# Folding the bias keys into the query weights on TensorE instead of on GpSimd and VectorE

## The chip, the cores and the metric

The kernel runs on one core of one Trainium2 chip. The metric is the device time of one execution in microseconds; lower is better. Before the change the median of three timed runs is 1137.2 us (1136.54 to 1137.88).

## What is computed

The reference is a chain of four cross-attention layers over a state `x` of 2 x 256 rows of 256 numbers and a context of 2 x 512 rows. The layer that matters here is L1: it holds two attentions of 16 heads of width 128, and each attention appends one learned "bias key" and "bias value" to the keys and values of every head.

```python
qh = (q_in @ wq + bq).reshape(b, q_len, H, K)          # H = 16 heads, K = 128
kh = jnp.concatenate([kh, jnp.broadcast_to(bias_k, (b, 1, H, K))], axis=1)
logits = jnp.einsum('bqhk,bthk->bhqt', qh, kh) / scale
```

The logit of the bias key is `q . bias_k[h]`, and `q` is linear in the layer's normed input. So a 256 x 16 matrix with one column per head, `folded[d, h] = sum_k wq[d, h, k] * bias_k[h, k]`, gives these logits from the input directly. It is needed once for each of the two attentions, and it depends on weights alone.

## The kernel before

The program is written by hand as a row of phases. Each phase owns its SBUF tiles and semaphores and ends in a barrier of all engines (line 131): nothing of the next phase, no load either, starts before the last instruction of this one. The phases are: transposes of the context, the narrow attention `L0a`, the MLP `L0m`, the two wide attentions `L1a` (more than half of the time), the MLP `L1m`, the narrow attention `L2a`, the narrow attention `L3a` and the MLP `L3m`.

The change lies in `L0m`, one of three phases that the function `mlp` writes. TensorE's work in `mlp` is a list of jobs, each into one of four PSUM banks in turn (the class `Ring`). Jobs 0 and 1 transpose the normed rows. Then come eight "up" jobs (m = 0 to 7), each six matmuls of 512 columns (lines 72 to 74) from the first weight matrix. ScalarE applies the gelu to each bank (`activated`, L849); VectorE splits the result into a high part (`hidden_hi`, a cast, L870) and a low part (`hidden_lo`, a subtraction, L871), and the second one frees the bank. Up job m may start only when VectorE has freed the bank of up job m - 4. Then come four "down" jobs, t = 0 to 3, of 24 matmuls of 256 columns each, and VectorE adds each to `x_rows` (L890). Every engine runs its own instructions strictly in order.

`L0m` alone also has the task of making `folded` for the next phase (`cfg["fold"]`, class `BiasKeyFold`). The query weights of an attention (2 MB) and its bias keys, broadcast over the 128 partitions (1 MB), are loaded; `fold.multiply` takes the product in place in pieces of 128 x 2048 (three pieces on GpSimd, the fourth on VectorE, L914), and `fold.reduce` on VectorE sums each piece over the width of a head (L919). VectorE's four reductions and its multiply stand between its MLP instructions. `L3m` is the same MLP with the same shapes, without the fold and without this neighbour work.

A second piece of code matters for reading the change. In the phase `L0a` the bias values are folded into the output weights by TensorE already: a tile `spread` of zeros, 32 columns per head, receives the head's vector in column c (L610); then 32 float32 matmuls of 32 weight columns and 256 moving columns (L435) put the 16 heads of each layer on four strips of 32 PSUM partitions.

Of the kernel before, what the change touches and what calls it, by code (L numbers as in the profile page):

```python
# [10 lines left out]
ALU = mybir.AluOpType  # L11
# [3 lines left out]
P = 128  # L15
# [3 lines left out]
D = 256  # L19
# [23 lines left out]
class Ring:  # L43


    def __init__(self, banks, sem, name):
        self.banks = banks
        self.n = len(banks)
        self.full = sem(f"{name}_full")
        self.hi_done = sem(f"{name}_hi_done")  # L50
        self.free = [sem(f"{name}_free{i}") for i in range(self.n)]
# [703 lines left out]
def mlp(nc, io, keep, cfg):  # L755

    with Phase(nc, cfg["name"]) as ph:
# [19 lines left out]
        w2 = [t[:, 4:8, :].rearrange("p s (g n) -> p (s g) n", g=2) for t in w]  # L777
        rows = keep[cfg["rows"]]
        up0 = KT
        down0 = up0 + FT + (len(context.jobs) if cfg["context"] else 0)  # L780

        @block.sync
        def _(sp):
            parts.load(sp, io)
            for i in range(4):
                sp.dma_start(stage[:, 2 * i:2 * i + 2, :], io[cfg["w"]][:, 2 * i:2 * i + 2, :]).then_inc(loaded[i], 16)
            sp.dma_start(b1[:, :], io[cfg["b1"]]).then_inc(small_loaded, 16)
            sp.dma_start(b2[:, :], io[cfg["b2"]].partition_broadcast(P)).then_inc(small_loaded, 16)
            if fold:
                fold.load(sp, io)  # L790
            if cfg["context"]:
                context.load(sp, io)
                sp.dma_start(context_rows[:, :, :], io["ctx_2048"].rearrange("b (t p) d -> p (b t) d", p=P)).then_inc(context_loaded, 16)
            if cfg["out"] is not None:
                for t in range(RT):
                    ring.wait_evacuated(sp, down0 + t)
                    sp.dma_start(io["out"].rearrange("b (t p) d -> p (b t) d", p=P)[:, t, :], keep["x"][:, t, :]).then_inc(stored, 16)
                sp.wait_ge(stored, 16 * RT)

        @block.gpsimd  # L800
        def _(pool):
            parts.root(nc, pool)
            if fold:
                fold.multiply(nc, pool, nc.gpsimd, fold.pieces[:3])
            if cfg["context"]:
                context.root(nc, pool)

        @block.tensor
        def _(pe):
            parts.transpose(nc, pe, ring, keep)  # L810
            for m in range(FT):
                job = up0 + m
                if m == 0:
                    ring.wait_evacuated(pe, 0)
                    ring.wait_evacuated(pe, 1)
                pe.wait_ge(w_lo, 4)
                ring.wait_bank(pe, job)
                for kt in range(KT):
                    last = product3(nc, ring.bank(job)[:, :], [t[:, kt, m * P:(m + 1) * P] for t in w1],
                                    [t[:, kt, :] for t in hT], kt == 0, kt == KT - 1)  # L820
                last.then_inc(ring.full, 1)
            if cfg["context"]:
                context.transpose(nc, pe, ring, keep)
            pe.wait_ge(w_lo, 8)
            for t in range(RT):
                job = down0 + t
                ring.wait_bank(pe, job)
                for f in range(FT):
                    if t == 0:
                        ring.wait_evacuated(pe, up0 + f)  # L830
                    last = product3(nc, ring.bank(job)[:, 0:D], [x[:, f, t * P:(t + 1) * P] for x in hidden],
                                    [x[:, f, :] for x in w2], f == 0, f == FT - 1)
                last.then_inc(ring.full, 1)

        @block.scalar
        def _(act):
            load_table(nc, keep, cfg["gelu"])
            for i in range(8):
                act.wait_ge(loaded[i // 2], 16)
                nc.scalar.copy(w[0][:, i, :], stage[:, i, :]).then_inc(w_hi, 1)  # L840
                if i == 3:
                    parts.scale(nc, act, ring)
            act.wait_ge(small_loaded, 32)
            for m in range(FT):
                job = up0 + m
                act.wait_ge(ring.full, job + 1)
                if m >= 4:
                    ring.wait_evacuated(act, job - 4)
                nc.scalar.activation(activated[:, m % 4, :], ring.bank(job)[:, :], cfg["gelu"],  # L849
                                     bias=b1[:, m:m + 1]).then_inc(ring.hi_done, 1)  # L850
            if cfg["context"]:
                context.scale(nc, act, ring)

        @block.vector
        def _(dve):
            link = Chain(dve, parts.dve_done)
            parts.normalise(nc, dve, link, rows, cfg["eps"], cfg["centred"])
            for i in range(8):
                dve.wait_ge(w_hi, i + 1)
                nc.vector.tensor_tensor(w[1][:, i, :], stage[:, i, :], raw(w[0][:, i, :]), ALU.subtract).then_inc(w_lo, 1)  # L860
                if i == 3:
                    parts.split(nc, dve, link, ring, hT)
            dve.wait_ge(small_loaded, 32)
            for t in range(RT):
                last = nc.vector.tensor_tensor(keep["x"][:, t, :], keep["x"][:, t, :], b2[:, :], ALU.add)
            link(last)
            for m in range(FT):
                job = up0 + m
                dve.wait_ge(ring.hi_done, up0 + m + 1)
                link(nc.vector.tensor_copy(hidden[0][:, m, :], activated[:, m % 4, :]))  # L870
                nc.vector.tensor_tensor(hidden[1][:, m, :], activated[:, m % 4, :], raw(hidden[0][:, m, :]),  # L871
                                        ALU.subtract).then_inc(ring.freed_by(job), 1)
                if cfg["context"] and m == 0:
                    context_link = Chain(dve, context.dve_done)
                    dve.wait_ge(context_loaded, 16)
                    context.statistics(nc, context_link, context_rows, 1e-5, True)
                if fold and m >= FT - 2:
                    fold.reduce(nc, dve, keep, *fold.pieces[m - FT + 2])
                if cfg["context"] and m == 3:
                    context.apply(nc, dve, context_rows, True)  # L880
            if cfg["context"]:
                context.split(nc, dve, context_link, ring, cfg["context"])
            if fold:
                fold.multiply(nc, dve, nc.vector, fold.pieces[3:])
            for t in range(RT):
                if fold and t < 2:
                    fold.reduce(nc, dve, keep, *fold.pieces[3 - t])
                job = down0 + t
                dve.wait_ge(ring.full, job + 1)
                nc.vector.tensor_tensor(keep["x"][:, t, :], ring.bank(job)[:, 0:D], keep["x"][:, t, :],  # L890
                                        ALU.add).then_inc(ring.freed_by(job), 1)


class BiasKeyFold:

    def __init__(self, ph):
        self.wq = [ph.sb(f"fold_wq{i}", [P, KT, H * DW]) for i in range(2)]
        self.bias_k = [ph.sb(f"fold_bias_k{i}", [P, H * DW]) for i in range(2)]  # L900
        self.loaded = [ph.sem(f"fold_loaded{i}") for i in range(2)]
        self.multiplied = [[ph.sem(f"fold_multiplied{i}{kt}") for kt in range(KT)] for i in range(2)]
        self.pieces = [(i, kt) for i in range(2) for kt in range(KT)]

    def load(self, sp, io):
        for i in range(2):
            sp.dma_start(self.bias_k[i][:, :], io[f"L1_bias_k{i + 1}"].partition_broadcast(P)).then_inc(self.loaded[i], 16)
            sp.dma_start(self.wq[i][:, :, :], io[f"L1_wq{i + 1}"].rearrange("(k p) n -> p k n", p=P)).then_inc(self.loaded[i], 16)

    def multiply(self, nc, engine, on, pieces):  # L910

        for i, kt in pieces:
            engine.wait_ge(self.loaded[i], 32)
            on.tensor_tensor(self.wq[i][:, kt, :], self.wq[i][:, kt, :], self.bias_k[i][:, :],  # L914
                             ALU.mult).then_inc(self.multiplied[i][kt], 1)

    def reduce(self, nc, dve, keep, i, kt):
        dve.wait_ge(self.multiplied[i][kt], 1)
        nc.vector.tensor_reduce(keep["folded"][:, i, kt, :], self.wq[i][:, kt, :].rearrange("p (h d) -> p h d", h=H),  # L919
                                AX.X, ALU.add)  # L920


def wide_attentions(nc, io, keep):
# [552 lines left out]
```

## Time and profile before

| what | value |
|---|---|
| median of three timed runs | 1137.2 us |
| time of the profiled execution | 1132.89 us |
| span of the profiled execution | 1131.1 us |
| TensorE (PE) busy | 956.8 us, 85% |
| VectorE (DVE) busy | 817.2 us, 72% |
| ScalarE (ACT) busy | 603.5 us, 53% |
| GpSimd (POOL) busy | 336.1 us, 30% |
| DMA moved | 69.49 MB, mean 61 GB/s |

The span runs from the first to the last instruction that the profiler recorded. Busy time of an engine is the time in which one of its instructions ran, whether it made progress or was held up inside. "Idle before" in a row is the time in which an engine waited ahead of that instruction, with an arrow to the instruction that released it. A float32 matmul shows as two records in the trace, a transpose as one.

### The profile page before, as it was taken

Reading aid. Unit: us, or ns where it says so; the run is one execution under the profiler, and the core shown is the slowest. Engines: PE = TensorE matmul, PEld = TensorE weight load, DVE = VectorE, ACT = ScalarE, POOL = GpSimd, SP = SyncE. Lnnn points to the kernel's source line nnn. Section 1 sums busy time; section 2 is a strip of 40 time slices with the busy share of each in tenths; the row PEclk is TensorE's granted clock in tenths of the full one; section 3 lists DMA queues with packets and bytes.
Section 4 is the critical chain, followed back from the end, with each engine's and each line's share of the span. In section 5 each row is a group of like instructions: output and inputs, shape, how many; then the busy total and the mean of one; then the engine's idle time right before and its main releaser. Section 6 shows DMA issues by size and latency. Waiting matters only on the chain. (4 is left out here: it accounts for less than half of the span.)

```text
span 1131.1 us, 17854 instructions
## 1 busy us (share of the span) xinstructions
PE 956.8 (85%) x6548; PEld 809.0 (72%) x6548; DVE 817.2 (72%) x1624; ACT 603.5 (53%) x1367; POOL 336.1 (30%) x325
## 2 busy tenths in 40 slices
PE   4888886569999999997899999998586898478958
PEld 3666665558888889887778989987475566465647
DVE  3377767976787878787578787877664787757865
ACT  2488873034555555553355555655424786257842
POOL 4255541441112222221111222200005454534520
PEclk8889997888999999998899999999788799688989
DMA  5984106140001111111000111000305930296120
GB/s 180 252 130 63 12 1 247 56 162 1 15 24 38 38 39 38 38 38 39 1 4 36 38 38 38 2 1 1 117 1 123 169 44 1 59 191 73 13 80 19
DMA packets 37810, 69.49 MB, mean 61 GB/s; under 512 B 7414, under 2 KB 23288, under 8 KB 35036
## 3 DMA queue, kind: packets, MB, share of 16 engines
q1 hardware_dynamic: 37724, 68.35, 24.7%
q8 instruction: 53, 0.87, 0.3%
q14 instruction: 33, 0.27, 0.1%
HBM read 57.31 MB, written 11.02 MB: 60 GB/s over the span
## 5 line engine op out<-in xcount | busy, mean ns | idle before, releaser
L1230 ACT CAST L1a_probsT_hi<-L1a_bank 128x512 fp32r<-128x512 f32 x128 | 68.8, 589 | 94.3 <-PE L1a_bank L1111 94.3
L1069 POOL TENSOR_SCALAR L1a_wo_hi<-L1a_stage 128x512 fp32r<-128x512 f32 x16 | 10.3, 646 | 363.2 <-PE L1a_sums L74 355.6
L1347 DVE TENSOR_REDUCE L1a_top<-L1a_scores 128x2 f32<-128x1024 f32 x64 | 78.2, 1222 | 36.1 <-PE L1a_scores L74 36.1
L1262 ACT ACTIVATE L1a_probs<-L1a_scores,L1a_neg_max 128x512 f32<-128x512 f32 x128 | 86.8, 684 | 30.6 <-DVE L1a_bias_shifted L1351 25.6
L1285 DVE TENSOR_TENSOR L1a_probsT_lo<-L1a_bank,L1a_probsT_hi 128x512 fp32r<-128x512 f32 x128 | 82.0, 682 | 0.1
L72 PE MATMUL L1a_bank<-L1a_probsT_hi,L1a_v_hi 128*128 128x256 f32 x256 | 73.2, 286 | 9.2 <-DVE L1a_probsT_lo L1285 9.2
L1232 ACT ACTIVATE L1a_attended_hi<-L1a_bank,L1a_cols 128x256 fp32r<-128x256 f32 x64 | 30.5, 476 | 90.4 <-PE L1a_bank L74 90.4
L72 PE MATMUL L1a_bank<-L1a_w_hi,ctxT_hi 128*128 128x256 f32 x256 | 76.5, 299 | 1.1 <-DVE latT_lo L1303 1.0
L74 PE MATMUL L1a_bank<-L1a_w_hi,ctxT_lo 128*128 128x256 f32 x256 | 73.7, 288 | 0.0
L73 PE MATMUL L1a_bank<-L1a_w_lo,ctxT_hi 128*128 128x256 f32 x256 | 73.6, 288 | 0.0
L390 POOL TENSOR_SCALAR L0a_probs<-L0a_probs,L0a_inverse 128x768 f32<-128x768 f32 x64 | 57.2, 906 | 52.9 <-DVE L0a_inverse L641 52.9
L73 PE MATMUL L1a_bank<-L1a_probsT_lo,L1a_v_hi 128*128 128x256 f32 x256 | 72.5, 283 | 0.0
L74 PE MATMUL L1a_bank<-L1a_probsT_hi,L1a_v_lo 128*128 128x256 f32 x256 | 72.5, 283 | 0.0
L627 DVE TENSOR_REDUCE L0a_neg_max<-L0a_scores 128x1 f32<-128x768 f32 x64 | 58.5, 955 | 17.9 <-PE L0a_scores L477 15.9
L1111 PE MATMUL L1a_bank<-ident,L1a_probs 128*128 128x128 f32 x512 | 66.3, 272 | 0.0
L1111 PEld LDWEIGHTS L1a_bank<-ident,L1a_probs 128*128 128x128 f32 x512 | 59.6, 140 | 8.3
L72 PE MATMUL L1a_scores<-L1a_k_hi,L1a_q_hi 128*128 128x512 f32 x128 | 52.9, 413 | 14.1 <-DVE L1a_v_lo L1285 7.2
L566 ACT ACTIVATE L0a_probs<-L0a_scores,L0a_neg_max 128x768 f32<-128x768 f32 x64 | 57.5, 909 | 10.6 <-DVE L0a_neg_max L627 10.6
L1287 DVE SCALAR_TENSOR_TENSOR L1a_attended_lo<-L1a_bank,L1a_cols,L1a_attended_hi 128x256 fp32r<-128x256 f32 x64 | 30.8, 482 | 39.3 <-ACT L1a_attended_hi L1232 38.4
L72 PE MATMUL L1a_bank<-ctxT_hi,L1a_w_hi 128*128 128x512 f32 x128 | 52.3, 409 | 7.2 <-DVE L1a_w_lo L1293 7.2
L72 PEld LDWEIGHTS L1a_bank<-L1a_probsT_hi,L1a_v_hi 128*128 128x128 f32 x256 | 49.1, 192 | 10.9 <-DVE L1a_probsT_lo L1285 10.7
L1362 DVE TENSOR_SCALAR L1a_probs<-L1a_probs,L1a_inverse 128x512 f32<-128x512 f32 x128 | 56.1, 480 | 0.0
(409 smaller groups left out, 3160.8 us busy)
## 6 DMA issues: line engine op xcount, KB each, us to landing
L1a_stage<-in_L_w SPq DMA_DIRECT2D x15, 1024.0 KB, 4.8
L0m_fold_wq<-in_L_wq SPq DMA_DIRECT2D x2, 2048.0 KB, 19.8
L0a_k_stack<-L0a_k_dram SPq DMA_DIRECT2D x12, 192.0 KB
L0a_w_qkv<-L0a_k_dram SPq DMA_DIRECT2D x12, 192.0 KB
L0a_probs<-in_L_wo SPq DMA_DIRECT2D x1, 2048.0 KB, 9.7
L0a_probsT<-in_L_wo SPq DMA_DIRECT2D x1, 2048.0 KB, 11.2
L0m_stage<-in_L_wm SPq DMA_DIRECT2D x4, 512.0 KB, 5.8
L0m_fold_bias_k<-in_L_bias_k SPq DMA_DIRECT2D x2, 1024.0 KB, 15.4
```

Of the source, the lines that this page charges most:

```text
L72: nc.tensor.matmul(out, lh, rh, start=start, stop=False, skip_group_check=loose)
L73: nc.tensor.matmul(out, lh, rl, start=False, stop=False, skip_group_check=loose)
L74: return nc.tensor.matmul(out, ll, rh, start=False, stop=stop, skip_group_check=loose)
L390: nc.gpsimd.tensor_scalar(probs[:, slot, :], probs[:, slot, :], inverse[:, small:small + 1], 1.0, ALU.mult, ALU.mult).then_inc(normed, 1)
L566: nc.scalar.activation(probs[:, m % probs_slots, :], slot_scores(m), ACT.Exp, bias=neg_max[:, small:small + 1], accum_out=row_sum[:, small ...
L627: nc.vector.tensor_reduce(neg_max[:, small:small + 1], slot_scores(m), AX.X, ALU.max, negate=True).then_inc(max_done, 1)
L1111: last = nc.tensor.transpose(ring.bank(job)[:, kt * P:(kt + 1) * P], probs[:, g % 2, qt, kt * P:(kt + 1) * P], keep["ident"][:, :])
L1230: nc.scalar.copy(out, source).then_inc(ring.hi_done, 1)
L1262: nc.scalar.activation(probs[:, g % 2, qt, :], scores[:, qt, :], ACT.Exp, bias=neg_max[:, g % 2, qt:qt + 1], accum_out=row_sum[:, g % 2, q ...
L1285: nc.vector.tensor_tensor(out[1], source, raw(out[0]), ALU.subtract).then_inc(ring.freed_by(job), 1)
L1347: link(nc.vector.tensor_reduce(top[:, :], scores[:, :, :], AX.X, ALU.max))
L1362: nc.vector.tensor_scalar(probs[:, s, qt, :], probs[:, s, qt, :], inverse[:, qt:qt + 1], None, ALU.mult).then_inc(normed, 1)
```

## The change

The product and the sum move to TensorE, in the form that `L0a` uses. The query weights come from HBM in another layout (head width on the partitions). GpSimd clears the `spread` tile; VectorE copies each key into its column after up job 2; TensorE runs 32 matmuls after up job 7 (job `fold_job`), ScalarE copies the result out, TensorE turns it by four transposes ahead of the last down job (job `turn_job`), and ScalarE picks the 16 used columns of each strip into `folded`. The broadcast loads of the keys, the four multiplies and the four reductions go.

```diff
         up0 = KT
-        down0 = up0 + FT + (len(context.jobs) if cfg["context"] else 0)
+        fold_job = up0 + FT
+        down0 = up0 + FT + (len(context.jobs) if cfg["context"] else 0) + (1 if fold else 0)
+        turn_job = down0 + RT - 1
...
             if fold:
+                fold.load_cols(sp, io)
                 fold.load(sp, io)
...
         def _(pool):
+            if fold:
+                nc.gpsimd.memset(fold.spread[:, :, :, :], 0.0).then_inc(fold.clear, 1)
             parts.root(nc, pool)
-            if fold:
-                fold.multiply(nc, pool, nc.gpsimd, fold.pieces[:3])
...
+            if fold:
+                ring.wait_bank(pe, fold_job)
+                fold.multiply(nc, pe, ring.bank(fold_job)).then_inc(ring.full, 1)
             pe.wait_ge(w_lo, 8)
             for t in range(RT):
-                job = down0 + t
+                if fold and t == RT - 1:
+                    ring.wait_evacuated(pe, fold_job)
+                    ring.wait_bank(pe, turn_job)
+                    fold.turn(nc, ring.bank(turn_job), keep["ident"][:, :]).then_inc(ring.full, 1)
+                job = down_job(t)
...
+            if fold:
+                act.wait_ge(ring.full, fold_job + 1)
+                nc.scalar.copy(fold.rows[:, :], ring.bank(fold_job)[:, :]).then_inc(ring.freed_by(fold_job), 1)
+                act.wait_ge(ring.full, turn_job + 1)
+                nc.scalar.copy(keep["folded"][:, :, :, :].rearrange("p i k (j c) -> p (i k) j c", c=4),
...
-                if fold and m >= FT - 2:
-                    fold.reduce(nc, dve, keep, *fold.pieces[m - FT + 2])
+                if fold and m == 2:
+                    fold.spread_keys(nc, dve)
...
-            if fold:
-                fold.multiply(nc, dve, nc.vector, fold.pieces[3:])
             for t in range(RT):
-                if fold and t < 2:
-                    fold.reduce(nc, dve, keep, *fold.pieces[3 - t])
-                job = down0 + t
+                job = down_job(t)
...
+    def load_cols(self, sp, io):
+        for i in range(2):
+            sp.dma_start(self.cols[i][:, :, :], io[f"L1_cols{i + 1}"]).then_inc(self.cols_loaded, 16)
...
     def load(self, sp, io):
         for i in range(2):
-            sp.dma_start(self.bias_k[i][:, :], io[f"L1_bias_k{i + 1}"].partition_broadcast(P)).then_inc(self.loaded[i], 16)
-            sp.dma_start(self.wq[i][:, :, :], io[f"L1_wq{i + 1}"].rearrange("(k p) n -> p k n", p=P)).then_inc(self.loaded[i], 16)
...
+            sp.dma_start(self.wq[i][:, :, :], io[f"L1_wqT{i + 1}"]).then_inc(self.loaded[i], 16)
+
+    def spread_keys(self, nc, dve):
+        dve.wait_ge(self.cols_loaded, 32)
+        dve.wait_ge(self.clear, 1)
+        for i in range(2):
+            for c in range(4):
+                last = nc.vector.tensor_copy(self.spread[:, i, c:H:4, c], self.cols[i][:, 1, c:H:4])
+        last.then_inc(self.ready, 1)
+
+    def multiply(self, nc, pe, bank):
+        pe.wait_ge(self.ready, 1)
+        for i in range(2):
+            pe.wait_ge(self.loaded[i], 16)
+            for c in range(4):
+                for j in range(4):
+                    h = 4 * j + c
+                    last = nc.tensor.matmul(bank[32 * j:32 * j + 32, i * D:(i + 1) * D], self.spread[:, i, h, :],
+                                            self.wq[i][:, h, :], start=c == 0, stop=c == 3)
+        return last
+
+    def turn(self, nc, bank, ident):
+        for x in range(2 * KT):
+            last = nc.tensor.transpose(bank[:, x * P:(x + 1) * P], self.rows[:, x * P:(x + 1) * P], ident)
+        return last
```

The first place is TensorE in `L0m`, at the end of up job 7 (`hT`, `w`: input and weights of the MLP; `hidden` feeds the down jobs) and in front of the last down job.

```order
 L73 MATMUL L0m_bank<-L0m_hT_lo,L0m_w_hi 128x512
 L74 MATMUL L0m_bank<-L0m_hT_hi,L0m_w_lo 128x512
+L947 MATMUL L0m_bank<-L0m_fold_wq,L0m_fold_spread 32x256 x32
 L72 MATMUL L0m_bank<-L0m_w_hi,L0m_hidden_hi 128x256
 L73 MATMUL L0m_bank<-L0m_w_lo,L0m_hidden_hi 128x256
...
 L74 MATMUL L0m_bank<-L0m_w_hi,L0m_hidden_lo 128x256
+L953 MATMUL L0m_bank<-ident,L0m_fold_rows 128x128 x4
 L72 MATMUL L0m_bank<-L0m_w_hi,L0m_hidden_hi 128x256
```

The 32 matmuls of the fold now stand between the last up job and the first down job, and the four transposes between the third and the fourth down job; nothing else of TensorE's order changes.

The second place is VectorE in `L0m`, from up job 6 to the end of the phase, first as it was.

```order
L870 CAST L0m_hidden_hi<-L0m_activated 128x512
L871 TENSOR_TENSOR L0m_hidden_lo<-L0m_activated,L0m_hidden_hi 128x512
L919 TENSOR_REDUCE folded<-L0m_fold_wq 128x16
L870 CAST L0m_hidden_hi<-L0m_activated 128x512
L871 TENSOR_TENSOR L0m_hidden_lo<-L0m_activated,L0m_hidden_hi 128x512
L919 TENSOR_REDUCE folded<-L0m_fold_wq 128x16
L914 TENSOR_TENSOR L0m_fold_wq<-L0m_fold_wq,L0m_fold_bias_k 128x2048
L919 TENSOR_REDUCE folded<-L0m_fold_wq 128x16
L890 TENSOR_TENSOR x_rows<-L0m_bank,x_rows 128x256
L919 TENSOR_REDUCE folded<-L0m_fold_wq 128x16
L890 TENSOR_TENSOR x_rows<-L0m_bank,x_rows 128x256 x3
```

And the same engine after the change, from up job 2 to up job 3, and then the end of the phase.

```order
L891 CAST L0m_hidden_hi<-L0m_activated 128x512
L892 TENSOR_TENSOR L0m_hidden_lo<-L0m_activated,L0m_hidden_hi 128x512
L937 COPY L0m_fold_spread<-L0m_fold_cols 128x4 x8
L891 CAST L0m_hidden_hi<-L0m_activated 128x512
L892 TENSOR_TENSOR L0m_hidden_lo<-L0m_activated,L0m_hidden_hi 128x512
...
L907 TENSOR_TENSOR x_rows<-L0m_bank,x_rows 128x256 x4
```

Five instructions of 128 x 2048 have gone from VectorE, and eight copies of four elements have come in behind up job 2.

## Rows read from the trace of the kernel before

**Rows 1.** Waits from 177 to 228 us: us in total, times, longest.
```profile
PE L0m_bank L72 <- DVE L0m_hidden_lo L871: 11.0, 3, 7.9
```

**Rows 2.** TensorE in order of time: start us, us, instruction, [idle before, releaser].
```profile
187.69 0.77 PE L72 MATMUL L0m_bank<-L0m_hT_hi,L0m_w_hi 128*128 128x512 f32 x1 [3.02 <-DVE L0m_hT_lo L752]
...
210.30 0.77 PE L72 MATMUL L0m_bank<-L0m_hT_hi,L0m_w_hi 128*128 128x512 f32 x1 [7.94 <-DVE L0m_hidden_lo L871]
```

**Rows 3.** VectorE in order of time, second half of `L0m`.
```profile
195.62 4.95 DVE L871 TENSOR_TENSOR L0m_hidden_lo<-L0m_activated,L0m_hidden_hi 128x512 fp32r<-128x512 f32 x1
200.50 4.76 DVE L870 CAST L0m_hidden_hi<-L0m_activated 128x512 fp32r<-128x512 f32 x1
...
210.07 0.41 DVE L870 CAST L0m_hidden_hi<-L0m_activated 128x512 fp32r<-128x512 f32 x1
210.52 0.69 DVE L871 TENSOR_TENSOR L0m_hidden_lo<-L0m_activated,L0m_hidden_hi 128x512 fp32r<-128x512 f32 x1
...
225.75 1.07 DVE L890 TENSOR_TENSOR x_rows<-L0m_bank,x_rows 128x256 f32<-128x256 f32 x3
```

**Rows 4.** Query by tile, the fold's weights: count, min/median/max ns, first and last start.
```profile
L919 DVE TENSOR_REDUCE folded<-L0m_fold_wq x4: 2274/2278/2286, 213.3 to 223.6; 128x16 f32<-128x2048 f32 x4
L914 POOL TENSOR_TENSOR L0m_fold_wq<-L0m_fold_wq,L0m_fold_bias_k x3: 4669/4697/4977, 195.3 to 204.9; 128x2048 f32<-128x2048 f32 x3
```

**Rows 5.** Stages: from:to, length, busy PE PEld DVE ACT POOL, clock, DMA share, GB/s.
```profile
210.00:213.00 3.00, 2.70 (x7) 2.18 (x8) 2.90 (x7) 0.00 (x0) 0.00 (x0) 0.50 0.03 5
...
186.50:195.30 8.80, 7.61 (x23) 6.08 (x24) 7.18 (x16) 3.63 (x7) 0.00 (x0) 0.65 0.98 413
...
202.60:210.00 7.40, 0.00 (x0) 0.00 (x0) 7.37 (x2) 0.48 (x1) 7.00 (x2) 0.75 0.00 0
```

**Rows 6.** `L3m` in order of time: first up matmul, first down matmul, last addition.
```profile
1103.31 0.76 PE L72 MATMUL L3m_bank<-L3m_hT_hi,L3m_w_hi 128*128 128x512 f32 x1 [3.55 <-DVE L3m_hT_lo L752]
...
1116.46 0.28 PE L72 MATMUL L3m_bank<-L3m_w_hi,L3m_hidden_hi 128*128 128x256 f32 x1
...
1128.02 0.42 DVE L890 TENSOR_TENSOR x_rows<-L3m_bank,x_rows 128x256 f32<-128x256 f32 x1 [2.41 <-PE L3m_bank L74]
```

**Rows 7.** The gelu of up job 2, in `L0m` and in `L3m`.
```profile
194.44 0.69 ACT L849 ACTIVATE L0m_activated<-L0m_bank,L0m_b 128x512 f32<-128x512 f32 x1 [0.71 <-PE L0m_bank L74]
...
1109.67 0.69 ACT L849 ACTIVATE L3m_activated<-L3m_bank,L3m_b 128x512 f32<-128x512 f32 x1 [0.71 <-PE L3m_bank L74]
```

**Rows 8.** The fold of the bias values in `L0a`: TensorE, ScalarE's copy, VectorE's spread.
```profile
47.93 1.93 PE L435 MATMUL L0a_bank<-L0a_probs,L0a_spread 128*32 128x256 f32 x32
49.68 1.91 PE L435 MATMUL L0a_bank<-L0a_probsT,L0a_spread 128*32 128x256 f32 x32
...
51.65 0.58 ACT L535 COPY bias_values<-L0a_bank 128x512 f32<-128x512 f32 x1 [2.97 <-PE L0a_bank L435]
...
40.47 0.69 DVE L610 TENSOR_TENSOR L0a_spread<-L0a_wide_cols 128x4 f32<-128x4 f32 x8
```

**Rows 9.** The second half of that fold as a stage (columns as in rows 5).
```profile
49.68:51.65 1.97, 1.91 (x36) 0.91 (x28) 0.00 (x0) 0.00 (x0) 0.00 (x0) 1.00 1.08 191
```

**Rows 10.** TensorE: eight transposes; four float32 matmuls of full width, and the next matmul.
```profile
848.32 1.07 PE L731 MATMUL L2a_bank<-ident,x_rows 128*128 128x128 f32 x8 [1.36 <-PEq L131]
...
521.04 1.89 PE L1149 MATMUL L1a_sums<-bias_values,L1a_bias_probsT 128*128 128x256 f32 x8
522.58 0.58 PE L72 MATMUL L1a_bank<-ctxT_hi,L1a_w_hi 128*128 128x512 f32 x1
```

**Rows 11.** GpSimd: the clearing of `spread` in `L0a`; the power of the norm in `L0m`.
```profile
L378 POOL MEMSET L0a_spread<- x1: 952/952/952, 27.7 to 27.7; 128x1024 f32 x1
...
180.44 1.03 POOL L702 TENSOR_TENSOR L0m_rstd<-L0m_shifted,L0m_power 128x4 f32<-128x4 f32 x1 [2.51 <-DVE L0m_shifted L112]
```

**Rows 12.** TensorE in `L1a`: neighbouring matmuls of 256 columns at half clock.
```profile
244.74 0.42 PE L73 MATMUL L1a_bank<-L1a_w_lo,ctxT_hi 128*128 128x256 f32 x1
244.95 0.41 PE L74 MATMUL L1a_bank<-L1a_w_hi,ctxT_lo 128*128 128x256 f32 x1
```

More of the change, by code:

```diff
@@ L779, in mlp, with down_job @@
         up0 = KT
-        down0 = up0 + FT + (len(context.jobs) if cfg["context"] else 0)
+        fold_job = up0 + FT
+        down0 = up0 + FT + (len(context.jobs) if cfg["context"] else 0) + (1 if fold else 0)
+        turn_job = down0 + RT - 1
+        def down_job(t):
+            return down0 + t + (1 if fold and t == RT - 1 else 0)
         @block.sync
@@ L795, in _ @@
                 for t in range(RT):
-                    ring.wait_evacuated(sp, down0 + t)
+                    ring.wait_evacuated(sp, down_job(t))
                     sp.dma_start(io["out"].rearrange("b (t p) d -> p (b t) d", p=P)[:, t, :], keep["x"][:, t, :]).then_inc(stored, 16)
@@ L852, in _ @@
                 context.scale(nc, act, ring)
+            if fold:
[3 more added lines that the diff above has]
+                nc.scalar.copy(keep["folded"][:, :, :, :].rearrange("p i k (j c) -> p (i k) j c", c=4),
+                               ring.bank(turn_job)[:, :].rearrange("p (x j r) -> p x j r", x=2 * KT, r=32)[:, :, :, 0:4]
+                               ).then_inc(ring.freed_by(turn_job), 1)
         @block.vector
@@ L898, in __init__ @@
     def __init__(self, ph):
-        self.wq = [ph.sb(f"fold_wq{i}", [P, KT, H * DW]) for i in range(2)]
-        self.bias_k = [ph.sb(f"fold_bias_k{i}", [P, H * DW]) for i in range(2)]
+        self.wq = [ph.sb(f"fold_wq{i}", [P, H, D]) for i in range(2)]
+        self.cols = [ph.sb(f"fold_cols{i}", [P, 4, H]) for i in range(2)]
+        self.spread = ph.sb("fold_spread", [P, 2, H, 32])
+        self.rows = ph.sb("fold_rows", [P, 2 * D])
         self.loaded = [ph.sem(f"fold_loaded{i}") for i in range(2)]
-        self.multiplied = [[ph.sem(f"fold_multiplied{i}{kt}") for kt in range(KT)] for i in range(2)]
@@ L903, in __init__ @@
-        self.pieces = [(i, kt) for i in range(2) for kt in range(KT)]
+        self.cols_loaded, self.clear, self.ready = ph.sem("fold_cols_loaded"), ph.sem("fold_clear"), ph.sem("fold_ready")
+    def load_cols(self, sp, io):
+        for i in range(2):
+            sp.dma_start(self.cols[i][:, :, :], io[f"L1_cols{i + 1}"]).then_inc(self.cols_loaded, 16)
     def load(self, sp, io):
         for i in range(2):
-            sp.dma_start(self.bias_k[i][:, :], io[f"L1_bias_k{i + 1}"].partition_broadcast(P)).then_inc(self.loaded[i], 16)
-            sp.dma_start(self.wq[i][:, :, :], io[f"L1_wq{i + 1}"].rearrange("(k p) n -> p k n", p=P)).then_inc(self.loaded[i], 16)
@@ L910, in multiply @@
[L910 to L920, printed above, removed]
+            sp.dma_start(self.wq[i][:, :, :], io[f"L1_wqT{i + 1}"]).then_inc(self.loaded[i], 16)
@@ L1462 @@
         t[f"L1_w{n}"] = np.concatenate(by_pair, axis=2)
-        t[f"L1_wq{n}"], t[f"L1_wo{n}"], t[f"L1_bias_k{n}"] = wq, wo, a[f"L1_xattn_bias_k{n}"].reshape(-1)
+        t[f"L1_wqT{n}"], t[f"L1_wo{n}"] = wq.reshape(D, H, DW).transpose(2, 1, 0), wo
         t[f"L1_cols{n}"] = np.stack([columns(a[f"L1_xattn_{m}{n}"].reshape(-1)) for m in ("bq", "bias_k", "bv", "bias_v")], axis=1)
```

## The prediction

> **What bounds the kernel now.** No single engine does: TensorE is busy 85% of the span and VectorE 72% (the table of the page above), so I looked at who waits for whom in the one phase that the change touches, `L0m`. I read four views in this order. The waits of that phase come first: TensorE waited three times for VectorE's low parts `hidden_lo`, 11.0 us in all, 7.9 us at once [rows 1]. TensorE in order of time gives the place: the long wait ends at 210.30, with up job 7, which needs the bank of up job 3 [rows 2]. VectorE in order of time gives the reason: from 195.62 to 210.07 it ran only three instructions, a low part of 4.95 us, a cast of 4.76 us and another low part. The same two kinds take 0.41 and 0.69 us right behind it [rows 3]. Last, the fold's own tile: GpSimd's three multiplies of 4.7 us each run from 195.3 to 204.9 + 4.7 = 209.6, exactly that stretch [rows 4]. It is not the loads that slow VectorE: from 202.6 on nothing was moved (0 GB/s), and VectorE crawled on until 210.07 [rows 5]. So each GpSimd multiply holds one VectorE instruction for its whole length. Behind 210 the fold costs once more: four reductions of 2.28 us and a multiply stand in VectorE's queue among the MLP's instructions [rows 4], and the last three additions come in one lump at the very end, 225.75 to 226.82 [rows 3]. The phase ends in a barrier, so what is saved in it moves everything behind it.
>
> **What the removal gives.** `L3m` is the same MLP without the fold. From its first up matmul, 1103.31, to the end of its last addition, 1128.02 + 0.42 = 1128.44, it takes 25.13 us [rows 6]. `L0m` takes 226.82 - 187.69 = 39.13 us between the same two points [rows 2, 3]. One difference is not the fold's: TensorE's clock rose later in `L0m`. The gelu of up job 2 starts 194.44 - 187.69 = 6.75 us behind the first matmul there, 1109.67 - 1103.31 = 6.36 us in `L3m` [rows 2, 6, 7], and no GpSimd multiply runs yet; that is 0.39 us. So `L0m` without any fold would take 25.52 us, and the old fold costs 39.13 - 25.52 = 13.6 us. As a check by parts: 11.0 us of waiting, half of the 3.0 us behind the wait in which the granted clock was 0.50 [rows 1, 5], and about 0.6 us for the lump of additions make 13.1 us.
>
> **What the new fold costs on TensorE.** The trace holds its twin: in `L0a` the 32 matmuls of 32 weight columns and 256 moving columns, in the same order over strips and with the same number format, start at 47.93, and ScalarE's copy of their result starts at 51.65, which is 3.72 us with both ends included [rows 8]. I take 3.72; the lower bound is twice the distance of its halves, 2 x 1.75 = 3.5 [rows 8]. The turn is four transposes; eight took 1.07 us in `L2a` [rows 10], so 0.53 us. Nothing hides these 4.25 us, since in the new order TensorE's queue has no wait left. The last up matmul ends at 187.69 + (1116.46 - 1103.31) + 0.39 = 201.23 [rows 2, 6], the fold at 204.95. Up job 7's low part is ready at about 201.23 + 0.2 + 0.69 + 1.06 = 203.2 [rows 3, 7], under the fold, so the down jobs start without a wait.
>
> A rule of the Trainium skill speaks for a dearer fold. "TensorE: Matmul & The Clock Gate", section on the measured speedup against the span model, gives 2.38 times for three column tiles, that is 79% of the ideal; and "TensorEngine Tiling (Array Packing)", Key Properties, says that a change of the tiling mode drains the engine. By that efficiency the estimate for four strips would be 12.3 / 3.17 = 3.9 us, and the sum below 0.2 us smaller. The twin's row contains its drains and gives 12.3 / 3.72 = 3.3 times, and I go by the row.
>
> **What is added beside it, at no cost.** GpSimd's clearing takes 0.95 us and stands ahead of the norm's power, in front of which GpSimd was idle for 2.51 us [rows 11]; without that cover it would delay the phase by at most 0.95. VectorE's eight small copies take 0.69 us in the twin [rows 8]. They stand behind up job 2, from about 196.3 to 197.0; up job 3 is then split by 198.1, and TensorE wants its bank for up job 7 at 201.23 - 1.40 = 199.8 (an up job takes 1.40 us at full clock: five from the gelu of job 2 to the first down matmul, less 0.2 [rows 6, 7]). VectorE needs 1.06 us for a job [rows 3], so it has caught up two jobs later. Uncovered, the copies would cost 0.69. ScalarE's copy of 0.58 us [rows 8] and the pick after the turn lie under down jobs of 2.84 us (24 of the 96 matmuls between 1116.46 and the last addition [rows 6]). The loads shrink by the two broadcasts: 4.2 MB and 64 KB of keys instead of 6.3 MB. The first 3.15 MB of before were there at 195.3 and came at 413 GB/s [rows 4, 5], so the fold's loads began near 187.7; the new ones land near 192.9 and 198.0, and TensorE wants them at 201.2 and 203.0. The slack is 5 us; to cost anything the rate would have to fall below 270 GB/s. The number of issues on SyncE stays at four, and no other queue is passed.
>
> **Sum.** -13.6 + 3.72 + 0.53 = -9.4 us. The phase would end at 226.82 - 9.4 = 217.4. The profiled execution took 1132.89 us with a span of 1131.1, so its like would take 1123.5 with a span near 1121.7. The median of the timed runs, 1137.2, lies 4.3 us above that profile for a reason that I can't read off it; the same 9.4 us off the median give **1127.8 us**.
>
> **The rivals.**
>
> *The strips don't run side by side.* Four float32 matmuls with full weights and 256 columns took 522.58 - 521.04 = 1.54 us, 0.385 each [rows 10]; 32 in a row would take 12.3 us, 8.6 more than the twin. The gain would be 0.8 us: 1136.4. For it speaks only that the fold reads other tiles; against it the twin with the same shapes. Chance 0.05. Half-way, a fold of twice the twin's time or a load that comes several us late, leaves 5.7 us: 1131.5, chance 0.07.
>
> *The clock falls behind the fold.* This is the case on the other side. TensorE works with 32 of its columns for 3.7 us, and if its clock sank to the half level at that and stayed there to the end of the phase, the 96 down matmuls would come at a pace of 0.21 instead of 0.118 us [rows 6, 12], 8.8 us more, the fold itself 3.7 more and the turn 0.5: 13.0 us against a gain of 9.4, so 3.6 us slower, 1140.8. It decides from 72% of that stretch at half clock on. For it: after the long wait of before the granted clock was 0.50 [rows 5]. Against it: in the twin's second half it was 1.00 [rows 9], and the new order takes TensorE's long idle stretch away. Chance 0.03. The Trainium skill has a rule on its side: "TensorE: Matmul & The Clock Gate", part on the PE-mode transpose, says that full clock does not engage for transposes, and four stand in this stretch. No row here shows transposes between dense matmuls.
>
> *More than the sum.* The idle stretch that goes may have been dearer in the timed runs than in the profiled one, 11 us or more: 1126 or below, chance 0.05. The phases behind start at other moments of the clock's pattern, which I can't forecast; the three runs of before differ by 1.3 us with that in them.
>
> **The numbers.** The likeliest case, 0.80, has a gain of 9.4 us. Its own bounds: the spread of the runs (0.7 us either way), and one stretch of about 2.7 us at half clock more or less, worth 1.35: 7.3 to 11.5, that is 1125.7 to 1129.9. The range that holds 8 in 10 goes a little into the half-way case: 1125.5 to 1130.6. About 0.2% (2.3 us) is what a measurement of this kernel can tell from no change. Faster by more: 0.80 + 0.07 + 0.05 = 0.92; the same: 0.05; slower: 0.03.
>
> **What would show each step.** After the change VectorE's low parts in `L0m` should all take 0.69 us and TensorE's wait for them in the up jobs should be near nothing. The 32 matmuls (64 records) should fill about 3.7 us at granted clock 1.00, from about 201 to 205. The phase should end near 217.4. The prediction is wrong if VectorE still crawls with GpSimd empty, if the fold takes over 7 us, if TensorE waits for the weights ahead of it, if the clock reads 0.50 behind it, or if the phase is 9 us shorter and the phases behind it are longer by as much.

## The result, and the profile after

The changed kernel took 1130.21 us in median (1125.32 to 1130.81, five runs) against 1136.54 us before (1134.11 to 1137.88, five runs). The medians differ by 6.3 us. The ratio, taken over all ten runs, is 0.9932, 95% interval 0.9904 to 0.996: 7.7 us less (0.0068 x 1136.54), with 4.5 to 10.9 inside the interval. The forecast was 9.4 us less and 1127.8 us, with a range of 1125.5 to 1130.6: the median lies inside the range, 0.4 us under its upper end, and 9.4 us lies inside the interval, so the times alone do not show that anything is missing.

The profiled execution took 1130.21 us with a span of 1128.4 us, only 2.7 us under the span of before, so I cut both traces at the barriers. These are differences between the first VectorE instructions of the phases (and the ends of the spans):

| phase | before | after | difference |
|---|---|---|---|
| up to `L0m` | 177.9 | 179.2 | +1.4 |
| `L0m` | 49.86 | 40.36 | -9.50 |
| `L1a` | 576.16 | 581.55 | +5.4 |
| `L1m` and `L2a` | 163.5 | 161.6 | -2.0 |
| `L3a` | 125.7 | 127.8 | +2.1 |
| `L3m` | 38.0 | 37.9 | -0.1 |

The changed phase gives what the sum said. Most of what is missing in this pair of profiles was lost in `L1a`, whose code is the same.

VectorE's low parts in `L0m`, by the query on their tile in the trace after, answer to [rows 3]: count, min/median/max ns, first and last start.

```profile
L892 DVE TENSOR_TENSOR L0m_hidden_lo<-L0m_activated,L0m_hidden_hi x8: 691/692/694, 193.3 to 203.9; 128x512 fp32r<-128x512 f32 x8
```

All eight take 0.69 us; none is held. The next rows are the trace after in order of time, for TensorE and then the other engines, as in [rows 2, 3, 8, 10, 11].

```profile
189.07 0.76 PE L72 MATMUL L0m_bank<-L0m_hT_hi,L0m_w_hi 128*128 128x512 f32 x1 [3.02 <-DVE L0m_hT_lo L752]
202.62 3.66 PE L947 MATMUL L0m_bank<-L0m_fold_wq,L0m_fold_spread 128*32 128x256 f32 x64
214.84 0.60 PE L953 MATMUL L0m_bank<-ident,L0m_fold_rows 128*128 128x128 f32 x4
...
197.52 0.67 DVE L937 COPY L0m_fold_spread<-L0m_fold_cols 128x4 f32<-128x4 f32 x8
...
218.31 0.42 DVE L907 TENSOR_TENSOR x_rows<-L0m_bank,x_rows 128x256 f32<-128x256 f32 x1 [2.85 <-PE L0m_bank L74]
...
179.20 0.96 POOL L810 MEMSET L0m_fold_spread<- 128x1024 f32 x1 [13.56 <-POOLq L131]
181.81 1.03 POOL L702 TENSOR_TENSOR L0m_rstd<-L0m_shifted,L0m_power 128x4 f32<-128x4 f32 x1 [1.61 <-DVE L0m_shifted L112]
```

The fold starts 13.55 us behind the first up matmul (forecast 201.23 - 187.69 = 13.54) and takes 3.66 us, the turn 0.60. No TensorE row between the first up matmul and the end of the phase has an idle time ahead of it, and from the fold on the granted clock was 1.00, as the stages show (columns as in [rows 5]):

```profile
202.00:206.00 4.00, 4.00 (x67) 2.18 (x66) 2.24 (x4) 0.70 (x2) 0.00 (x0) 1.00 0.00 0
206.00:218.00 12.00, 12.00 (x108) 11.79 (x100) 1.27 (x3) 0.80 (x2) 0.00 (x0) 1.00 0.01 1
```

Now the start of `L1a`. There VectorE adds `out_bias` to `x_rows` (four additions, two SBUF inputs each; L1325, after the change L1359) and then splits the keys (`k_lo`), for which TensorE's next job waits, while GpSimd prepares the output weights (`wo`) and the second set of weights (`w`, L1060 and L1094). First the trace of before:

```profile
238.40 2.94 DVE L1325 TENSOR_TENSOR x_rows<-x_rows,L1a_out_bias 128x256 f32<-128x256 f32 x4
241.27 2.71 DVE L1287 SCALAR_TENSOR_TENSOR L1a_k_lo<-L1a_bank,L1a_bk,L1a_k_hi 128x512 fp32r<-128x512 f32 x4
243.90 3.32 DVE L1302 CAST latT_hi<-L1a_whole 128x512 fp32r<-128x512 f32 x1
...
243.47 3.46 POOL L1060 TENSOR_TENSOR L1a_w_lo<-L1a_stage,L1a_w_hi 128x1536 fp32r<-128x1536 f32 x1
...
242.15 1.22 PE L731 MATMUL L1a_bank<-ident,L1a_normed 128*128 128x128 f32 x8 [1.53 <-DVE L1a_k_lo L1287]
```

And the same place after:

```profile
231.74 6.62 DVE L1359 TENSOR_TENSOR x_rows<-x_rows,L1a_out_bias 128x256 f32<-128x256 f32 x4
238.28 2.71 DVE L1321 SCALAR_TENSOR_TENSOR L1a_k_lo<-L1a_bank,L1a_bk,L1a_k_hi 128x512 fp32r<-128x512 f32 x4
...
233.86 3.46 POOL L1094 TENSOR_TENSOR L1a_w_lo<-L1a_stage,L1a_w_hi 128x1536 fp32r<-128x1536 f32 x1
...
239.16 1.94 PE L731 MATMUL L1a_bank<-ident,L1a_normed 128*128 128x128 f32 x8 [7.08 <-DVE L1a_k_lo L1321]
```

It is the collision of `L0m` again. Before, the additions were nearly through when GpSimd began its second set, and the long GpSimd instruction (3.46 us) held a cast that TensorE hardly needed (its waits there were 0.2 and 0.8 us). After, the second set started while the additions ran: one addition took 1.68 us and the next 3.63 us instead of 0.42. The four take 6.62 us instead of 2.94, and TensorE waits 7.08 us instead of 1.53 and comes back at half clock (granted clock 0.50 from 235 to 241 us, against 1.00 in the same place before; eight transposes in 1.94 us instead of 1.22). GpSimd's first weight work of the phase waits for a load, here before and then after:

```profile
238.52 0.79 POOL L1069 TENSOR_SCALAR L1a_wo_hi<-L1a_stage 128x512 fp32r<-128x512 f32 x1 [7.61 <-DMA L1a_stage<-in_L_w]
...
228.94 1.14 POOL L1103 TENSOR_SCALAR L1a_wo_hi<-L1a_stage 128x512 fp32r<-128x512 f32 x1 [6.15 <-DMA L1a_stage<-in_L_w]
```

### The profile page after: what moved, and what is told of

Its sections match the earlier page's. It is cut to its first block and busy times, and to the rows that moved or that the text cites. A ratio compares the mean times of both kernels' runs of the same rounds, so it can differ in the third digit from the quotient of the medians.

```text
span 1128.4 us, 17996 instructions
## 1 busy us (share of the span) xinstructions
PE 961.3 (85%) x6616; PEld 813.0 (72%) x6616; DVE 798.5 (71%) x1627; ACT 605.1 (54%) x1369; POOL 322.8 (29%) x323
## 5 line engine op out<-in xcount | busy, mean ns | idle before, releaser
L1103 POOL TENSOR_SCALAR L1a_wo_hi<-L1a_stage 128x512 fp32r<-128x512 f32 x16 | 10.7, 668 | 362.2 <-PE L1a_sums L74 356.1
L72 PEld LDWEIGHTS L1a_bank<-L1a_probsT_hi,L1a_v_hi 128*128 128x128 f32 x256 | 49.0, 192 | 10.9 <-DVE L1a_probsT_lo L1319 10.6
```

The source lines that it names most:

```text
L72: nc.tensor.matmul(out, lh, rh, start=start, stop=False, skip_group_check=loose)
```

## The experiments

The theory, P: what counts in both phases is which VectorE instruction meets a GpSimd instruction; at the start of `L1a` that depends on the moment at which a load lands, and the gain in the times is that of `L0m` plus or minus this. The rival, C: the phases behind `L0m` merely start at another moment of TensorE's clock pattern. The kernel before ran next to each group of experiments: 1135.14 us in median next to the first three, 1134.88 next to the following four, 1131.95 next to the next four, 1135.54 next to the last. `L0m` repeats within 0.9 us between profiles of one kernel, while the times of one kernel spread over several us; so for `L0m` the phases decide, and the times stand beside them. The long phases repeat less well, as the table further down shows.

**after_again.** No edit.

> The changed kernel once more. Its runs so far lie in two groups, 1125.3 and 1126.0 us on one side, 1130.2 to 1130.8 on the other. Theory P (port lottery): at the start of L1a GpSimd's work on the second weight set and VectorE's four additions of out_bias to x_rows meet by chance, and who comes first depends on when a load lands; so the runs fall into two groups some 5 us apart again, and a profile of the slow group shows the additions at over 6 us in all and TensorE waiting about 7 us for k_lo, one of the fast group near 2.9 us and 1.5 us. Theory C (clock pattern): the phases behind L0m start at another moment of the clock's pattern; then the times spread evenly between 1125 and 1131, and the additions' length does not go with the time.

Measured: 1127.81 us (1125.15 to 1131.69, six runs), ratio 0.9933 (0.9906 to 0.9959). The times lie at 1125.2, 1125.2, 1127.2, 1128.4, 1131.0 and 1131.7: no two clean groups. The profile has `L0m` 40.33 and `L1a` 581.71 us, additions 6.62 us, TensorE's wait 7.54 us. The mechanism is there again, but the times alone do not show the two groups that theory P expected.

**q_before and q_after.** One line in GpSimd's program of `L1a`, in the kernel before and in the changed one:

```diff
                 else:
                     pool.wait_ge(first_loaded[3], 16)
+                    ring.wait_evacuated(pool, job_of["norm1", 0])
```

> The kernel before, with one wait added: in L1a GpSimd starts its first weight work only when VectorE has split layer 0's normed rows, so the two can't meet at the additions and the k splits. Theory P: the runs lie within 1 us of each other and at or under the fast end of before, 1130 to 1134 us; the additions take 1.4 us. Theory C: the spread stays 2 to 4 us and the median stays 1136 to 1137 (or rises, if GpSimd's second weight set now comes late).

> The changed kernel with the same wait. Theory P: within 1 us of each other, 9.4 us under q_before in median (25.52 + 4.25 us for L0m against 39.13), so 1121 to 1125 us. Theory C: still two groups or a spread of 5 us, and a difference to q_before of 6 to 8 us as it was between the two kernels.

Measured: q_before 1129.73 us (1125.69 to 1133.15, twelve runs), ratio to before 0.9952 (0.9929 to 0.9975); q_after 1115.71 us (1114.31 to 1116.72, five runs), ratio 0.9823 (0.98 to 0.9846). The start of `L1a` in q_after:

```profile
229.75 1.43 DVE L1360 TENSOR_TENSOR x_rows<-x_rows,L1a_out_bias 128x256 f32<-128x256 f32 x4
231.10 2.72 DVE L1322 SCALAR_TENSOR_TENSOR L1a_k_lo<-L1a_bank,L1a_bk,L1a_k_hi 128x512 fp32r<-128x512 f32 x4
...
236.12 0.62 POOL L1104 TENSOR_SCALAR L1a_wo_hi<-L1a_stage 128x512 fp32r<-128x512 f32 x1 [14.46 <-DVE latT_lo L1338]
```

`L1a` now takes 572.10 us in q_before and 571.50 in q_after: a wait added to GpSimd saves 3 to 4 us against the better start (575.06 and 576.16 in two profiles of before) and 10 against the other, and the difference between the two kernels in that phase has shrunk to 0.6. `L0m` takes 50.06 and 39.96. So P holds for the place. Its second claim, runs within 1 us of each other, fails: q_before still spreads over 7.5 us. Its time for q_after, 1121 to 1125 us, was missed too, by 5 us. The gap between the two in the times, 14.0 us, is larger than the 10.1 + 0.6 us of these two phases; in the two profiles the rest lies mostly in the phases behind (`L1m` and `L2a` 163.86 and 162.62, `L3a` 125.86 and 123.79), which the change does not touch and which vary as much between profiles of one kernel (below). What makes the gap that large in the times is not shown.

**serial_strips.** q_after with the fold's inner loops exchanged, so that the matmuls of one strip follow each other:

```diff
-            for c in range(4):
-                for j in range(4):
+            for j in range(4):
+                for c in range(4):
                     h = 4 * j + c
```

> q_after with the two inner loops of the fold exchanged: the four matmuls of one strip of 32 PSUM partitions follow each other, then the next strip. If the fold is cheap because four strips run side by side, the 32 matmuls now take about 12 us instead of 3.7, TensorE works through it with no cover, and the kernel takes 8 to 9 us more than q_after: about 1124 us. If it is the count of instructions that sets its pace, nothing changes: 1115.7.

Measured: 1122.24 us (1118.8 to 1122.95, four runs), ratio to before 0.9888 (0.9845 to 0.9931); `L0m` 44.61 us.

```profile
201.87 8.17 PE L947 MATMUL L0m_bank<-L0m_fold_wq,L0m_fold_spread 128*32 128x256 f32 x64
```

The fold goes from 3.66 to 8.17 us and the phase grows by 4.65. The granted clock was 1.00 in both, so the order over the strips is what counts: they do run side by side in the changed kernel, and losing it costs 4.5 us, not the 8.6 that I had put on it: matmuls of 32 weight columns in one strip come every 0.255 us (8.17 / 32), not every 0.385 as those with full weights [rows 10].

**gp_multiply and gp_clear.** q_after with GpSimd work that nothing waits for, in `L0m`, started behind up job 1; in gp_clear the line in the loop clears the tile, eight times.

```diff
+                ring.wait_evacuated(pool, up0 + 1)
+                for n in range(3):
+                    nc.gpsimd.tensor_tensor(fold.lone[:, :], fold.lone[:, :], fold.lone[:, :], ALU.mult).then_inc(fold.lone_set, 1)
```

> q_after with three multiplies of 128 x 2048 on GpSimd, of a tile that nothing else touches, started when up job 1 is split, as in the kernel before; no load, no reduction and nothing of the fold depends on them. If a GpSimd multiply holds VectorE's instruction, three VectorE instructions of 4.7 us come back, TensorE waits about 9 to 10 us in the up jobs, and the kernel takes 9 to 11 us more than q_after: about 1125.5. If the old fold's price was VectorE's own reductions or its loads, the time stays within 1 us of 1115.7.

> The same with eight clears of that tile by GpSimd in place of the three multiplies, some 15 us of work that writes SBUF and reads nothing. If any GpSimd work holds VectorE, 8 to 11 us more than q_after. If it is the reading of SBUF that collides with VectorE's second input, the low parts (two inputs) stay at 0.69 us and at most the casts are held: 0 to 3 us more.

Measured: gp_multiply 1127.77 us (1124.59 to 1131.71, ten runs), `L0m` 50.79 us, 10.8 more than q_after. VectorE and GpSimd in its trace:

```profile
197.10 3.79 DVE L898 CAST L0m_hidden_hi<-L0m_activated 128x512 fp32r<-128x512 f32 x1 [0.25 <-ACT L0m_activated L870]
200.92 3.97 DVE L899 TENSOR_TENSOR L0m_hidden_lo<-L0m_activated,L0m_hidden_hi 128x512 fp32r<-128x512 f32 x1
204.81 4.06 DVE L946 COPY L0m_fold_spread<-L0m_fold_cols 128x4 f32<-128x4 f32 x8
...
197.00 11.35 POOL L817 TENSOR_TENSOR L0m_fold_lone<-L0m_fold_lone 128x2048 f32<-128x2048 f32 x3 [12.00 <-DVE L0m_hidden_lo L899]
...
205.03 0.76 PE L72 MATMUL L0m_bank<-L0m_hT_hi,L0m_w_hi 128*128 128x512 f32 x1 [4.50 <-DVE L0m_hidden_lo L899]
210.07 0.77 PE L72 MATMUL L0m_bank<-L0m_hT_hi,L0m_w_hi 128*128 128x512 f32 x1 [2.14 <-DVE L0m_hidden_lo L899]
```

Three multiplies hold a cast, a low part and one of the copies of four elements, each for its own length. TensorE waits 6.6 us for low parts, not the 9 to 10 expected, and its granted clock was 0.50 from 205 to 213 us behind the first wait. Both kernels also have a clear that fills the extra tile at the start of the phase, and it met VectorE's normed rows:

```profile
183.28 2.65 DVE L716 TENSOR_SCALAR L0m_normed<-sum_rows,L0m_rstd 128x256 f32<-128x256 f32 x4 [1.22 <-POOL L0m_rstd L702]
```

They take 1.14 us in q_after, and the first up matmul starts 1.1 us later in the phase. So 1.1 us of the difference is that clear's, and 9.7 us come from the three multiplies: with nothing else of the old fold in the kernel, most of its price is back. gp_clear took 1123.4 us (1118.86 to 1124.38, four runs), `L0m` 44.87 us, 4.9 more than q_after, of which 1.1 us is that first clear's and 3.8 the eight clears'. Its casts and low parts by tile:

```profile
L898 DVE CAST L0m_hidden_hi<-L0m_activated x8: 426/1380/2102, 194.2 to 210.1; 128x512 fp32r<-128x512 f32 x8
L899 DVE TENSOR_TENSOR L0m_hidden_lo<-L0m_activated,L0m_hidden_hi x8: 691/692/693, 194.7 to 211.5; 128x512 fp32r<-128x512 f32 x8
```

The clears hold the casts (median 1.38 us instead of 0.43) and never a low part. The small copies into `spread` were held too, 1.20 us for the eight instead of 0.67. The expectation of 0 to 3 us more was too low: six casts are held, and TensorE waits 1.9 us for a low part that stands behind them. That the low parts themselves would stay free was right.

**no_fold.** q_after with one transpose of `ident` in place of the 32 matmuls and one in place of the turn's four; it leaves out the bias keys' logits.

> q_after with one transpose in place of the fold's 32 matmuls and one in place of the four of the turn; the loads, the spread and ScalarE's copies stay, and the bias keys' logits are not computed. The prediction put 4.25 us on the fold and the turn, all of it on the path: 4.0 us under q_after, 1111.7 us, with the phase L0m at about 36 us instead of 40. If part of it were hidden under VectorE's last low parts, 3 us or less.

Measured: `L0m` 36.30 us, 3.66 less than q_after (4.0 expected). The times, 1110.27 to 1117.83 in four runs with median 1114.13, spread too far to show 4 us.

**before_2, before_3 and after_3.** No edit; one execution each, for the profile.

> The kernel before, profiled again, to see what its start of L1a does. Theory P: its phase L0m is 50 us long as before (49.9), and L1a is either 576 us (the additions under 3 us in all) or about 581.5 us (the additions 6.6 us), by when the last piece of the first weights lands. If it is 576 us each time, the slower start belongs to the changed kernel and takes 5 of its 9.5 us back for good.

> The kernel before a third time, same question and same values as for before_2.

> The changed kernel a third time: L0m 40.3 us, and L1a 581.6 us as in both profiles so far if the slower start is its own, 575 to 576 us if it is a lottery and this run is of the 1125 us group.

| profile | `L0m` | `L1a` | additions | wait for `k_lo` | `L3a` | time |
|---|---|---|---|---|---|---|
| before | 49.86 | 576.16 | 2.94 | 1.53 | 125.7 | 1132.89 |
| before_2 | 49.69 | 581.77 | 6.33 | 7.48 | 124.4 | 1137.4 |
| before_3 | 50.55 | 575.06 | 2.93 | 2.00 | 125.7 | 1135.12 |
| after | 40.36 | 581.55 | 6.62 | 7.08 | 127.8 | 1130.21 |
| after_again | 40.33 | 581.71 | 6.62 | 7.54 | 125.5 | 1131.69 |
| after_3 | 40.04 | 581.24 | 6.62 | 6.38 | 121.3 | 1122.27 |

The kernel before has both starts, so the costly one does not belong to the change; but the changed kernel had it three times of three. GpSimd's first weight work in `L1a` began 10.8 us into the phase in the two better cases and 9.3 to 10.5 us in the four others, so the costly start goes with a load that lands earlier. Six profiles show that the two go together; no run moved the landing by itself. Over the three profiles of each kernel the means are: `L0m` 9.8 us shorter after the change, `L1a` 3.8 us longer, the phases behind it 1.2 us shorter, the span 7.1 us shorter. Rival C is not empty either: after_3 has the costly start and is yet the shortest of its kernel, because its `L3a` took 6.6 us less than that of the first profile. There the granted clock reached 1.00 a stage earlier; whether this is the cause or a sign of something else in `L3a` is not shown, for no experiment was made there. First after_3, then the first profile after, stages 45 us into `L3a`:

```profile
1006.36:1021.36 15.00, 13.97 (x111) 9.56 (x113) 13.69 (x32) 13.63 (x38) 9.51 (x14) 1.00 0.89 109
```
```profile
1007.67:1022.67 15.00, 12.42 (x79) 8.21 (x79) 9.67 (x21) 10.02 (x27) 7.37 (x11) 0.73 1.10 120
```

**quieter.** q_after with two more waits of GpSimd in `L1a`:

```diff
                     pool.wait_ge(loaded[j], 16 * (p // 2 + p % 2))
+                    if p % PAIRS == 2:
+                        pool.wait_ge(normed, 2 * (p // PAIRS) * GL + 2)
...
                     parts[1].root(nc, pool)
+                    ring.wait_evacuated(pool, job_of["norm1", 1])
```

> q_after with GpSimd also held back at two more places of L1a: its work on the third weight set of each layer starts after the first unit's softmax, and its work on the output weights at the start of the second layer after the split of the normed rows. In q_after VectorE's negation of the bias scores takes 2.3 us of which 1.3 are held, and the normed rows 1.7 us too long, with TensorE waiting behind. If these are on the path, 2 to 4 us under q_after: 1112 to 1114 us; if TensorE has slack there, the same as q_after.

Measured: 1111.64 us (1111.22 to 1113.8, four runs), ratio to before 0.9824 (0.9791 to 0.9856); `L1a` 569.70 us, 1.8 less than in q_after. In the whole of `L1a`, TensorE's waits at the two places shrank from 4.6 to 2.9 us (`k_lo`) and from 4.3 to 2.5 us (`neg_bias_scores`), but those for `probsT_lo` grew from 9.2 to 11.5. The seven other kernels that have the first wait lie between 570.19 and 572.10 us in this phase, so a gain of 1.8 us is no more than they differ among themselves: that the two waits are worth something is likely, but not shown. By the ratios it is the same as q_after (0.9823).

**all_vector.** q_before with the old fold wholly on VectorE:

```diff
-                fold.multiply(nc, pool, nc.gpsimd, fold.pieces[:3])
...
             for t in range(RT):
+                if fold:
+                    fold.multiply(nc, dve, nc.vector, fold.pieces[t:t + 1])
+                    fold.reduce(nc, dve, keep, *fold.pieces[t])
```

> q_before with the old fold wholly on VectorE: GpSimd multiplies nothing, and VectorE multiplies and reduces one piece ahead of each of the four additions at the end of L0m. TensorE's order is that of before. The work on VectorE grows from 11.4 to 18.3 us, but none of it collides. If the collision was the old fold's price, TensorE no longer waits in the up jobs, VectorE is the last to end, and L0m takes about 46 us against 50 in q_before and 40 in q_after. If the amount of work was the price, L0m takes 50 us or more.

Measured: 1121.64 us (1119.86 to 1122.79, four runs), ratio to before 0.987 (0.9838 to 0.9903); `L0m` 45.13 us, 4.9 less than q_before. TensorE has no wait in its jobs, and VectorE ends last, with this chain four times over:

```profile
218.43 2.28 DVE L909 TENSOR_TENSOR L0m_fold_wq<-L0m_fold_wq,L0m_fold_bias_k 128x2048 f32<-128x2048 f32 x1
220.75 2.29 DVE L914 TENSOR_REDUCE folded<-L0m_fold_wq 128x16 f32<-128x2048 f32 x1
222.95 0.41 DVE L885 TENSOR_TENSOR x_rows<-L0m_bank,x_rows 128x256 f32<-128x256 f32 x1
```

So half of the gain in `L0m` needs no TensorE at all: all of the work leaves GpSimd, and VectorE's reductions all stand behind its last low part, where one had stood between those of up jobs 6 and 7. The edit changes both at once; what GpSimd's multiplies alone cost, gp_multiply shows. The move to TensorE gives the other half (45.13 to 39.96).

## Why the prediction was right, and where it was not

The terms of the sum hold, each by its own measurement. That the time as a whole fell into the range is in part luck: the profile of before that the sum starts from had the better start of `L1a`, that of after the costly one, and `L1a` took back 5.4 us of 9.5 in this pair. The median, 1130.21, lies just outside the likeliest case's own bounds (1125.7 to 1129.9); the repeat of the changed kernel gave 1127.81.

- **What the removal gives (13.6 us).** Held. no_fold has `L0m` at 36.30 us, 13.56 under the first profile of before (13.4 and 14.3 under the other two), with two transposes still in it. The reason, that a GpSimd multiply holds one VectorE instruction for its length, is shown by gp_multiply and from the other side by all_vector.
- **What the new fold costs (3.72 and 0.53 us).** Held: 3.66 and 0.60, and 3.66 by leaving both out except for two transposes, against 4.0. The twin was the right row. The estimate from the Trainium skill's figure ("TensorE: Matmul & The Clock Gate", section on the measured speedup against the span model) was 3.9, 0.2 above the measured one.
- **What is added at no cost.** Held: GpSimd was still idle for 1.61 us ahead of the norm's power, the spread copies took 0.67 us with no wait of TensorE behind them, and TensorE did not wait for the weights, which landed by 199.4, ahead of the fold at 202.62.
- **The end of `L0m`.** Forecast 9.4 us earlier, measured 9.50, 9.53 and 9.82 in the three profiles of after against the first of before, and 9.3 to 10.5 over all nine pairs.
- **"The strips don't run side by side".** It did not happen. Its price was mis-sized: 4.5 us instead of 8.6 (serial_strips).
- **"The clock falls behind the fold".** It did not happen: 1.00 through fold, turn and down jobs, and the four transposes of the turn did not bring it down.
- **The phases behind.** This is the step that was too simple. I had written that the phases behind start at other moments of the clock's pattern and put 1.3 us on them. In the profiles the start of `L1a` alone is worth 5 to 6 us, by a second collision of the two engines that the trace of before held and that I did not follow beyond the barrier, and `L3a` varies by 6.6 us. The prediction's own last sign of being wrong, the phase 9 us shorter and the phases behind it longer by as much, came true by a little over half in the first pair of profiles (9.5 shorter, 5.4 longer). The gain in the times, 7.7 us, is under 9.4, as that would make it, but the interval holds 9.4 as well.

What stays open: whether the changed kernel always draws the costly start of `L1a` (three profiles of it and three of before can't tell), what moves the landing of that load, what makes `L3a` shorter in after_3, and why q_before and q_after differ by 14.0 us in the times and by 10.7 in the two phases.

## What to carry to other kernels

When an instruction of VectorE takes several times its usual length, look at what GpSimd runs at that moment before anything else. Moving the work to TensorE or to VectorE, or a wait that only parts the two engines, paid here, even though in all_vector VectorE had more work of its own than before. The wait that parted them in `L1a` cost one line and gave back more there than had been lost there: q_after and quieter, at 0.982 of the time of before, beat both kernels. And after a saving ahead of a barrier, compare the phases behind it one by one, since a meeting that depends on a load's landing can take back half of it in one run and nothing in another.

## What the runs showed of the hardware

- A GpSimd multiply of 3.8 or 4.7 us held casts, two-input subtractions and even a copy of four elements for its own length (gp_multiply; [rows 3, 4] for the first two). Clears held casts (1.38 us instead of 0.43), small copies (1.20 us for eight instead of 0.67) and the normed rows (2.65 us for four instead of 1.14), but no subtraction (gp_clear). The Trainium skill, "SBUF — State Buffer", section "Who interferes with whom", says that a VectorE instruction with two SBUF inputs collides with a GpSimd instruction that reads SBUF and not with one that only writes it. It also says that copies, casts and operations with a scalar can enter a mode in which they take the port pair that VectorE shares with GpSimd. The traces agree: 3.97 us against 0.69 for the low part beside the multiplies, 0.69 beside the clears, and 1.38 for the cast beside the clears.
- The multiply of a tile by itself took GpSimd 3.8 us (11.35 / 3), that of two tiles 4.7 [rows 4].
- Float32 matmuls of 32 weight columns and 256 moving columns came every 0.11 us with the strips in turn (3.66 / 32) and every 0.255 us within a strip (8.17 / 32), against 0.385 us with full weights [rows 10], all at full clock.
